# Delta rule: where PE puts the state's queries in a slot, and the transposed keys in the first slots

## What is computed

```python
q = silu(conv(x @ Wq)); k = silu(conv(x @ Wk)); v = silu(conv(x @ Wv))     # causal, 4 taps
alpha = sigmoid(x @ Wa + ba); beta = sigmoid(x @ Wb + bb)
def step(S, inp):
    qt, kt, vt, at, bt = inp
    err = einsum('bhvk,bhk->bhv', S, kt) - vt
    S = at * S - bt * err * kt
    return S, einsum('bhvk,bhk->bhv', S, qt)
o = layernorm(o) * ln_w + ln_b
o = (o * sigmoid(x @ Wg)) @ Wo
```

## Time and profile before

| | us |
|---|---|
| median of 3 runs | 3294.53 |
| lowest, highest | 3293.99, 3295.24 |
| the profiled execution, its own time | 3290.8 |
| its span, first to last instruction | 3288.9 |
| attention and first routed step, up to about | 647 |
| fill of the delta rule | 793 to 944 |
| full slots | about 1000 to 2887 |

### The profile page before, as it was taken

The page is one execution under the profiler, slowest core; times in us unless marked ns, Lnnn a source line. Parts: engine busy times, 40 slices in busy tenths (PEclk is TensorE's granted clock), DMA queues, the critical chain, the costliest instruction groups (busy, mean ns, idle before and its releaser), DMA issues.

```text
span 3288.9 us, 60848 instructions
## 1 busy us (share of the span) xinstructions
PE 2928.9 (89%) x19888; PEld 2424.0 (74%) x19888; DVE 2503.2 (76%) x6373; ACT 2093.2 (64%) x4556; POOL 1808.7 (55%) x1913
## 2 busy tenths in 40 slices
PE   4999999945669999999999999999999999987863
PEld 3777777734558888888888888888888888865652
DVE  4556665574668788788888888888888888889986
ACT  2555655523447777777777777777777777754531
POOL 1111111132677667676676767768676686766442
PEclk9999999957889999999999999999999999989985
DMA  2000000002575656746656566566666566543311
GB/s 94 1 0 0 0 0 0 1 26 74 162 201 165 194 181 176 208 142 200 199 165 197 159 195 194 163 195 177 181 188 184 174 176 196 162 131 91 102 34 51
DMA packets 572119, 422.72 MB, mean 129 GB/s; under 512 B 228691, under 2 KB 475219, under 8 KB 571734
## 3 DMA queue, kind: packets, MB, share of 16 engines
q1 hardware_dynamic: 571862, 419.51, 44.0%
HBM read 276.39 MB, written 143.01 MB: 128 GB/s over the span
## 4 chain that ended last, share of the span: by engine, by line
PE 73%; DVE 12%; POOL 7%; ACT 3%; issue 3%; DMA 1%; SPq 0%; DVEq 0%; POOLq 0%; ACTq 0%
PE bank L1987 25%; PE bank L2038 15%; PE bank L2135 6%; PE bank L1841 5%; POOL oT L805 4%; PE bank L2043 3%; PE bank L1753 3%; PE bank L1816 3%; PE bank L1826 3%; PE bank L2018 2%; PE bank L2026 1%; ACT oT L1092 1%; DVE acc L1534 1%; PE bank L1795 1%; PE bank L1811 1%
## 5 line engine op out<-in xcount | busy, mean ns | idle before, releaser
L772 POOL TENSOR_TENSOR acc<-acc,shifted 128x510 f32<-128x510 f32 x384 | 585.6, 1527 | 553.7 <-DVE acc L1534 550.5
L1534 DVE SCALAR_TENSOR_TENSOR acc<-bank,conv_w,acc 128x254 f32<-128x254 f32 (+1 forms) x1536 | 628.6, 471 | 98.5 <-ACT acc L1022 95.1
L1987 PE MATMUL bank<-x_k,w_kq 128*128 128x256 f32 x2048 | 503.6, 391 | 13.0 <-DMA x_k<-xT_scratch 8.9
L1020 ACT ACTIVATE shifted<-bank,conv_w 128x255 f32<-128x255 f32 x768 | 367.0, 478 | 217.9 <-issue 147.3
L1022 ACT ACTIVATE acc<-bank,conv_b,conv_w 128x256 f32<-128x256 f32 x768 | 439.9, 573 | 0.0
L1987 PEld LDWEIGHTS bank<-x_k,w_kq 128*128 128x128 f32 x2048 | 378.4, 194 | 80.8 <-issue 31.8
L789 POOL TENSOR_TENSOR inv<-inv,outer 128x30 f32<-128x30 f32 (+14 forms) x480 | 258.4, 538 | 37.6
L2135 PE MATMUL bank<-w_o,oT 128*128 128x256 f32 x1024 | 246.3, 385 | 33.5 <-POOL oT L805 33.5
L786 POOL TENSOR_TENSOR outer<-inv 128x30 f32<-128x30 f32 (+14 forms) x480 | 236.2, 492 | 30.6 <-DMA inv<-L_scratch 2.8
L1987 PE MATMUL bank<-x_g,w_g 128*128 128x256 f32 x1024 | 251.1, 389 | 0.0
L2018 PE MATMUL bank<-kq 128*128 128x256 f32 x1024 | 244.4, 382 | 5.1 <-ACT kq L1032 4.0
(11 more groups left out here) (235 smaller groups left out, 6539.9 us busy)
## 6 DMA issues: line engine op xcount, KB each, us to landing
abc<-decay_scratch SPq DMA_DIRECT2D x64, 512.0 KB, 6.0
q_scratch<-kq SPq DMA_DIRECT2D x64, 512.0 KB, 6.9
L_scratch<-LM SPq DMA_DIRECT2D x64, 512.0 KB, 3.5
M_scratch<-LM SPq DMA_DIRECT2D x64, 512.0 KB, 6.7
LTm<-L_scratch SPq DMA_DIRECT2D x64, 512.0 KB, 4.5
MTm<-M_scratch SPq DMA_DIRECT2D x128, 256.0 KB, 4.3
kqm<-q_scratch SPq DMA_DIRECT2D x64, 512.0 KB, 4.1
k_scratch<-knw SPq DMA_DIRECT2D x64, 258.0 KB, 4.8
```

The lines of the kernel that those rows point to most:

```text
L772: pool.tensor_tensor(dst, dst, shifted[:, u % 2, :, 1:], ALU.add).then_inc(Z["sumk" if u < 4 else "sumv"], 1)
L1020: act.activation(shifted[:, u % 2, i % 2, 1:], pj[:, 0:SEQ - 1], ACT.Copy, scale=conv_w[:, kind, bass.ds(head, 1), TAPS - 2:TAPS - 1].rear ...
L1534: dve.scalar_tensor_tensor(out=acc[:, kind, i, t:], in0=pj[:, 0:SEQ - t], scalar=wcol, in1=acc[:, kind, i, t:], op0=ALU.mult, op1=ALU.add) ...
L1987: mm = pe.matmul(dst[:, i * SEQ:(i + 1) * SEQ], w[:, k, head * DK:(head + 1) * DK], x[:, k, :], start=(k == 0), stop=(k == CT - 1))
```

## The change

Two edits in the order of PE's program; nothing is added or removed.

- In full slots `queries_on_state()` moves from between `keys(p)` and `outT` to between `products(p, 2)` and `project_out(0)`.
- In fill slots 1 to 7 `keys(s - 1)` moves from ahead of `proj_k(0)` to behind `proj_k(2)`.

```diff
                 if s < FILL:
-                    if s > 0:
-                        keys(s - 1)
                     proj_k(0), proj_k(1), proj_k(2)
                     if s > 0:
-                        products(s - 1, 0), products(s - 1, 1), products(s - 1, 2)
+                        keys(s - 1), products(s - 1, 0), products(s - 1, 1), products(s - 1, 2)
                     proj_k(3)
...
                     if pre:
                         keys(p)
-                    if middle:
-                        queries_on_state()
                     if rear:
                         outT(0), outT(1)
                     if pre:
                         products(p, 0), products(p, 1), products(p, 2)
+                    if middle:
+                        queries_on_state()
                     if rear:
                         project_out(0)
```

## The result

The changed kernel takes 3304.43 us (median of 14 runs, 3299.02 to 3308.08), against 3294.68 (14 runs, 3288.94 to 3296.59) beside it: ratio 1.003, interval 1.0023 to 1.0037. It is slower by 0.3%. That is inside the range, but it is not the case I held likeliest; it is the second rival in a mild form, plus a piece that no part of the prediction priced.

A forecast was written before the change was run, and what follows sets the result against it. PE was taken to bound the full slots. Full slots 0, the queue behind the queries 0 and the fill +2.3 took the median from 3294.53 to 3296.8 us; range 3290 to 3314.

The forecast's parts named there:

- the case I held likeliest: Whole kernel: nothing moves in the full slots, the fill gets a little slower; chance 0.63.
- the second rival: Fourth full slots: BDN lands 2.2 us late behind load_q, 13 times, giving 3326, or 3311 at half; chance 0.26.
- PE's own chain and POOL's: Full slots: two chains to the output projection; POOL's gated product still ends with DVE's scan, so sum 0.
- a new wait instead of the old: Full slots: PE waits 0.54 us for DVE's normalised output ahead of the output's transposes.
- L2135 <- POOL: PE's wait before the output projection for POOL's gated output: to drop from 33.5 to under 10 us.
- What is queued behind the queries: SP's queue in full slots: load_q about 4 us later, BDT and BDN behind it; taken 0, ends 0 and +29.
- My explanation of the slow issue by the earlier weights: Fourth slot: DMA engines full with earlier-issued weights made BDN's four pieces take 3.06 us to issue, against 1.86 in a quiet slot.
- My full price: Fourth slots: BDN 2.2 us late by plainly shifted rows, 13 times, 29 us.
- Fill: Fill slots: -0.4 from slot 1, +1.3 for transposed keys in slots 2 to 4, +1.4 for the clock; sum +2.3.
- The clock's term of 1.4: Fill slot 3: 4 us of unbroken idleness lowers PE's clock, costing 1.7 us at odds of 4 in 5.
- The wait simply goes: Full slots: the projection gains 0.47 us in 41 slots and 0.92 in 13, 31 us, giving 3266; chance 0.11.
- BDN comes late: Fourth slots, behind load_q: 2.2 us by 13 gives 3326, half of it 3311; chance 0.26.

## Why the prediction was right and where it failed

- **PE's own chain and POOL's (full slots, 0).** Right, step by step: the start of the transposes and that of the projection to 0.01 us, the gated pair's end, the group of four at 139.1 wherever BDN is not late (139.14 to 139.19 in the changed kernel with load_q last). That PE has a new wait instead of the old is in every run with the queries moved. Its size was 0.38 us, not 0.54; the sum did not depend on it. L2135 <- POOL fell to 1.8 us over the whole span.
- **What is queued behind the queries (0 taken, 0 to 29 as ends).** This step failed. I shifted the rows by 4.4 us, which was right (4.50). Then I let the queue give back 3.4 of them, so that the last piece of BDN would be issued near 2050 and land near 2052, 1 us before PE wants it. In the slot of 2031, less 2.28, it was issued at 2051.12 and landed at 2053.07: 2.4 us came back, 0.7 in the issue of BDT and 1.7 at the landing, none in the issue of BDN (3.15 us against 3.06, where I had expected it nearer to the 1.86 of a quiet slot). That the DMA engines would have less to do was right for the stretch of the earlier trace rows, moved by 2.3, and it ends before BDN is issued. While the four pieces were issued the engines were full again, as they were in slot 63 of the kernel before (columns as in the earlier trace rows; two stretches of the changed kernel, then slot 63 before):

```profile
2039.30:2050.30 11.00, 10.16 (x66) 9.10 (x65) 9.60 (x17) 8.58 (x15) 10.59 (x6) 1.00 0.79 276
...
2050.78:2053.93 3.15, 3.15 (x23) 2.48 (x22) 1.94 (x4) 0.95 (x3) 0.00 (x0) 1.00 1.00 355
...
2878.74:2881.84 3.10, 2.18 (x12) 1.70 (x11) 2.65 (x7) 2.40 (x6) 2.26 (x2) 1.00 0.99 357
```

  Share 0.79 instead of 1.05 ahead of the issue, and 1.00 in it. My explanation of the slow issue by the earlier weights was a reading that no row had tested, and a row of the kernel before speaks against it. Slot 63 loads no new weights for keys and queries, its last weights are issued at 2869.70, and the four pieces still take 3.10:

```profile
2875.88 1.81 SPq L473 DMA_DIRECT2D BDT<-inv_scratch  x4
...
2878.74 3.10 SPq L473 DMA_DIRECT2D BDN<-invT_scratch  x4
```

  The rival was to be decided by a last landing later than 2053.18 in the slot of 2031. By that it missed narrowly (2053.07), and the cover of 1 us that I had counted was 0.1. In 10 of the other 12 fourth slots BDN did come late, by 0.2 to 1.5 us, most in the slot of 1334, where SP lost 1.5 us more in the issue of BDT: 7.1 us in all, with slot 9. My full price was too high because it kept 3.7 us from the last issue to the landing; in the two slots shown it was 1.95 and 2.04.
- **The store at the slot's end.** Not in the prediction at all, so a zero without a reason: I asked who waits for BDT and BDN, and for the stores behind them asked nobody. 3.2 us in the drain. With BDN's 7.1 this is 10.3, near the 9.8 between the medians.
- **Fill (+2.3).** The 0.44 us per slot is there (16.71 against 16.27) and slot 1 gives back about 1.1 instead of my 0.4 (from the fill's start to the projections of slot 2: 31.24 us in the run with the queries alone, 30.13 in the one with the keys alone). Together they are near zero, as measured. The clock's term of 1.4 was wrong: I took one execution for the old order, and five of its seven profiled executions have slot 3 at 7.1 us or more. The rule of the Trainium skill that I named (TensorE: Matmul & The Clock Gate, "Loop structure matters more than you think") is neither borne out nor refuted here: with 4 us of idleness in one piece the projections took 7.1 us every time, with the same broken by the keys 5.42, 7.11 or 7.9.
- **The rivals.** "The wait simply goes" is refuted, and its reason against it was the right one. "BDN comes late" was the case, at a quarter of its full price, at 0.26. That the time fell inside the range is owed to this rival, whose half price set the upper end; the value that I took, 3296.8, is 7.6 us under the measured one. Without the fill's 2.3 and with the 10.3 of the queue the same sum gives 3304.8, against 3304.43.

## What to carry to other kernels

When a piece of work moves later, look up every DMA that waits for it, and then every DMA behind that one in the queue, to the end of the slot and into the last slot, where other code waits for the stores. Take the plain shift of the rows as the likeliest value; a queue that is said to catch up needs a row that shows it catching up. A load that must wait goes behind those that are due earlier, if it is not itself due: one place in SP's order removed the whole loss. A wait of 0.5 us in every slot can have a second one under it, which here was hidden by the very work that was moved. And a term that rests on the clock in one execution should be looked up in another before it is counted.

## What the runs showed of the hardware

- The standstill of POOL beside DVE's scan is not peculiar to the gated product: POOL's product of 128x168 took 2.42 us beside the scan against about 0.5 for its neighbours, and the scan 2.45. Nor, as these rows read, to the scan. In the changed kernel's slot 63 POOL's `add_shifted` (1.27 us by itself) began just behind DVE's last product of the normalisation and lasted until about 1 us after the scan:

```profile
2879.05 1.21 DVE L1625 TENSOR_TENSOR o<-o,ors 128x1024 f32<-128x1024 f32 x1
2879.20 4.33 POOL L772 TENSOR_TENSOR acc<-acc,shifted 128x510 f32<-128x510 f32 x1 [0.28 <-DVE acc L1534]
2880.18 2.29 DVE L1543 TENSOR_TENSOR_SCAN dec<-abc,inject 128x1032 f32<-128x1032 f32 x1
```

  In the ordinary full slot the two share the loss: `add_shifted` took 2.18 us, and the scan, which began while it ran, 3.38.
- Four DMAs of 32 KB took 2.3 to 3.3 us to issue in the fourth slots of the kernel before and 2.3 to 3.75 in those of the changed one, mostly about 3.1. In the other full slots, which have no stores of the inverses ahead of them, they mostly took 1.86, but over 2.2 in 4 of 40 before (2.77 in the slot of 1962) and in 11 of 40 after (2.81 at 1386.98). What makes the difference stays open. The two stores of 512 KB stand directly ahead of BDN in the fourth slots, and the DMA engines were full during its issue (share 0.99 to 1.07) against 0.39 in the quiet slot of 1997; but the 2.81 at 1386.98 came at a share of 0.55, and a run without the stores was not made.
- The time of the fill differs by 5 us between executions of the same code (166.4 to 171.4 us), and the projections of slot 3 come at either level of the clock.
